# Fused attention and slot network on one core: the first attention's loop runs over pairs of sequences, and the next input is transposed one group earlier

## The reference, cut to what matters

```python
x = x + _L0_attn_a_ref(_layernorm(x, axis=-1), wq, wk, wv, wo)   # x: (16, 256, 128)
...
q = jnp.einsum('bsd,hed->bhse', x, wq)      # the same for k and v
scores = jnp.einsum('bhse,bhte->bhst', q, k) / scale
scores = jnp.where(causal_mask, NEG, scores)
weights = jax.nn.softmax(scores, axis=-1)
heads = jnp.einsum('bhst,bhte->bhse', weights, v)
return concat @ wo.T
```

## Time and profile before

| | |
|---|---|
| median of 3 runs | 973.76 us (971.58 to 976.4) |
| profiled execution | 972.47 us, span 970.7 us |
| PE busy | 799.1 us (82% of the span) |
| DVE, ACT, POOL busy | 682.4, 472.6, 408.9 us |

### The profile page before, as it was taken

One profiled execution on the slowest core, in us unless ns is written; L12 is line 12 of the kernel. 1 busy time (PEld: TensorE's weight loads), 2 busy tenths in 40 slices (PEclk: granted clock), 3 DMA queues, 4 the chain that ended last, 5 costly groups with the idle time before them and its releaser, 6 DMA issues.

```text
span 970.7 us, 25469 instructions
## 1 busy us (share of the span) xinstructions
PE 799.1 (82%) x10228; PEld 614.3 (63%) x10228; DVE 682.4 (70%) x1560; ACT 472.6 (49%) x801; POOL 408.9 (42%) x302
## 2 busy tenths in 40 slices
PE   2899999999999999999995876668888888839655
PEld 1687777877788777877774453534555555525434
DVE  4677666676666766676664776548999999967763
ACT  1667666676666766776661423023333433315220
POOL 1445444444455444454442100018877778851000
PEclk9999999999999999999997977679999999957786
DMA  6000000000000000000000000000111111120002
GB/s 264 2 3 1 0 0 0 0 0 0 0 0 0 0 0 0 0 0 0 1 2 2 1 0 1 1 1 11 17 18 20 22 22 18 20 27 1 1 1 87
DMA packets 71586, 13.17 MB, mean 14 GB/s; under 512 B 66432, under 2 KB 70528, under 8 KB 70912
## 3 DMA queue, kind: packets, MB, share of 16 engines
q1 hardware_dynamic: 71552, 12.71, 6.0%
HBM read 8.51 MB, written 4.19 MB: 13 GB/s over the span
## 4 chain that ended last, share of the span: by engine, by line
PE 67%; DVE 19%; issue 6%; ACT 5%; POOL 3%; DMA 1%; DVEq 0%; SPq 0%; ACTq 0%; POOLq 0%
PE PS L525 6%; PE PS L482 6%; PE PS L341 6%; PE PS L342 5%; PE PS L343 5%; PE PS L418 4%; DVE b_prod L811 4%; PE PS L704 3%; PE PS L518 3%; PE PS L713 3%; PE PS L504 3%; PE PS L508 2%; PE PS L506 2%; PE PS L695 2%; PE PS L489 2%
## 5 line engine op out<-in xcount | busy, mean ns | idle before, releaser
L626 POOL TENSOR_TENSOR a_pl<-a_p,a_ph 128x1024 f16<-128x1024 f32 (+1 forms) x128 | 210.4, 1644 | 273.5 <-ACT a_ph L551 273.5
L858 POOL TENSOR_TENSOR b_w<-b_v,b_e 128x2048 f32<-128x2048 f32 x32 | 137.7, 4306 | 6.8 <-ACT b_e L773 6.8
L548 ACT ACTIVATE a_p<-PS 128x1024 f32<-128x1024 f32 (+1 forms) x128 | 103.8, 811 | 75.6 <-PE PS L489 75.5
L593 DVE TENSOR_REDUCE a_nm<-PS 128x4 bf16<-128x512 f32 (+1 forms) x128 | 121.3, 947 | 0.0
L541 ACT ACTIVATE a_qk_h<-PS 128x512 f16<-128x512 f32 x128 | 73.3, 604 | 79.5 <-PE PS L343 78.6
L551 ACT ACTIVATE a_ph<-PS 128x1024 f16<-128x1024 f32 (+1 forms) x128 | 103.0, 804 | 0.0
L811 DVE TENSOR_TENSOR b_prod<-PS,b_qt 128x512 f32<-128x512 f32 x128 | 83.0, 678 | 15.8 <-PE PS L697 15.0
L341 PE MATMUL PS<-xh,a_wqk_h 128*128 128x256 f16 x256 | 70.8, 277 | 27.1 <-DVE xl L577 26.9
L582 DVE TENSOR_TENSOR a_qk_l<-PS,a_qk_h 128x512 f16<-128x512 f32 x128 | 87.0, 681 | 2.8 <-ACT a_qk_h L541 2.8
L364 POOL TENSOR_TENSOR veps<-mv,eps 128x2 f32<-128x2 f32 (+2 forms) x40 | 7.9, 198 | 189.4 <-DVE mv L1132 137.1
L695 PE MATMUL PS<-b_kh,w_rolls 128*128 128x256 f16 x256 | 64.7, 281 | 20.6 <-DVE b_prod L811 19.7
(11 more groups left out here) (220 smaller groups left out, 2060.7 us busy)
## 6 DMA issues: line engine op xcount, KB each, us to landing
scratch_dram<-b_o SPq DMA_DIRECT2D x32, 64.0 KB, 3.5
b_y<-scratch_dram SPq DMA_DIRECT2D x16, 128.0 KB, 2.1
out_dram<-X SPq DMA_DIRECT2D x2, 1024.0 KB, 3.9
w_rest<-rest_dram SPq DMA_DIRECT2D x1, 1846.0 KB, 14.6
X<-x_dram SPq DMA_DIRECT2D x1, 1792.0 KB, 10.7
w_first<-first_dram SPq DMA_DIRECT2D x1, 1600.0 KB, 6.6
w_rolls<-rolls_dram SPq DMA_DIRECT2D x1, 512.0 KB, 15.2
X<-x_dram SPq DMA_DIRECT2D x1, 256.0 KB, 3.1
```

What stands on the lines that cost most here:

```text
L548: act.activation((a_p0, a_p1)[j][:, me, :, :, :].rearrange("p a h q -> p a (h q)"), TT[:, :, 0:512 - 256 * j], ACT.Exp, scale=EA ** -0.5)
L593: dve.tensor_reduce(a_nm[:, nx, j, :].rearrange("p (a h) -> p a h", a=2)[:, :, 0:2], MM[:, :, 0:256 * (j + 1)].rearrange("p a (h k) -> p a ...
L626: pool.tensor_tensor(*(n[:, g % 2, :, :, :].rearrange("p a h q -> p (a h q)") for n in (pl, p, ph)), ALU.subtract).then_inc(a_split, 1)
L858: pool.tensor_tensor(b_w8[:, j, :, :, :], rolled_values(par, j, 0, H), rolled_exps(par, j, 0, H), ALU.mult).then_inc(b_weighed, 1)
```

## The change

The loop's body becomes a pair of sequences (`a_steps(0) + a_steps(1)`), run 6 times; sequences 0 and 1 stand written out ahead of it, 14 and 15 behind it. In a step, g now runs from 0 to 7, and its high bit is the parity of the sequence. `xh` and `xl` of the first attention become `a_xhs` and `a_xls` with two slots, the sequence's parity choosing the slot. `norm` moves from group 1 to group 0, `apply` from group 2 to group 1, and `xt` from the end of group 2 to the end of group 1, ahead of `project`.

```diff
-def a_steps(first=False, last=False):
+def a_steps(par, first=False, last=False):
...
-        put(g == 2 and not last, ("apply", 0))
+        put(g == 1 and not last, ("apply", 0))
...
-        put(g == 1 and not last, ("norm", 0))
+        put(g == 0 and not last, ("norm", 0))
...
-        put(g == 2 and not last, ("xt", 0))
+        put(g == 1 and not last, ("xt", 0))
         put(g == 1 and not first, ("project", 0))
...
-A_PLAN = [(A_PROLOGUE, -1, None), (a_steps(first=True), 0, None), (a_steps(), 1, NB - 2),
-          (a_steps(last=True), NB - 1, None), (A_EPILOGUE, NB, None)]
+A_PLAN = [(A_PROLOGUE, -1, None), (a_steps(0, first=True) + a_steps(1), 0, None),
+          (a_steps(0) + a_steps(1), 1, NB // 2 - 2), (a_steps(0) + a_steps(1, last=True), NB // 2 - 1, None),
+          (A_EPILOGUE, NB // 2, None)]
...
+        a_xhs, a_xls = sb("a_xhs", [128, 2, SEQ], F16), sb("a_xls", [128, 2, SEQ], F16)
...
+        def parts(b_par, g):
+
+            slot = 1 - b_par if g == GA - 1 else b_par
+            return a_xhs[:, slot, :], a_xls[:, slot, :]
...
-                    act.activation(xh[:, :], src[:, 0:SEQ], ACT.Copy).then_inc(a_xh, 1)
+                    act.activation(a_xhs[:, 1 - b_par, :], src[:, 0:SEQ], ACT.Copy).then_inc(a_xh, 1)
```

More of the change, by code:

```diff
@@ L75, in put @@
         def put(cond, *new):
-            steps.extend((kind, g, n) for kind, n in new if cond)
+            steps.extend((kind, GA * par + g, n) for kind, n in new if cond)
         put(prepare, ("qk", 0), ("qk", 1))
@@ L134, in b_steps @@
     return steps
-A_PROLOGUE = [("norm", 3, 0), ("apply", 3, 0), ("xt", 3, 0), ("qk", 3, 0), ("qk", 3, 1), ("lo", 3, 0),
-              ("lo", 3, 1), ("masks", 3, 0), ("max", 3, 0), ("v", 3, 0), ("vlo", 3, 0), ("masks", 3, 1), ("max", 3, 1)]
+A_PROLOGUE = [("norm", 7, 0), ("apply", 7, 0), ("xt", 7, 0), ("qk", 7, 0), ("qk", 7, 1), ("lo", 7, 0),
+              ("lo", 7, 1), ("masks", 7, 0), ("max", 7, 0), ("v", 7, 0), ("vlo", 7, 0), ("masks", 7, 1), ("max", 7, 1)]
 A_EPILOGUE = [("normal", 0, 0), ("turn", 0, 0), ("pv", 0, 0), ("pv", 0, 1), ("normal", 1, 0), ("turn", 1, 0),
@@ L404, in a_read @@
             kind, g, j = step
+            b, g = 2 * b + g // GA, g % GA
             u = GA * b + g
@@ L420, in causal, with do @@
                               skip_group_check=True)
+        def parts(b_par, g):
+            slot = 1 - b_par if g == GA - 1 else b_par
+            return a_xhs[:, slot, :], a_xls[:, slot, :]
         def a_tensor(pe):
-            def do(step, b, fill):
+            def do(step, i, fill):
                 kind, g, j = step
+                b_par, b, g = g // GA, 2 * i + g // GA, g % GA
                 u = GA * b + g
@@ L439, in do @@
                         pe.wait_ge(a_xl, b + 2)
+                    xh, xl = parts(b_par, g)
                     for z in range(2):
                         ins = mm3(pe, dst[:, z * SEQ:(z + 1) * SEQ], a_wqk_h[:, pair, z, :], a_wqk_l[:, pair, z, :],
-                                  xh[:, :], xl[:, :], z == 0, z == 1)
+                                  xh, xl, z == 0, z == 1)
                     ins.then_inc(a_filled, 1)
@@ L511, in do @@
                 elif kind == "turn":
-                    if isinstance(b, int) and b == 0 and g == GA - 1:
+                    if isinstance(i, int) and b == 0 and g == GA - 1:
                         pe.wait_ge(w_loaded, 16 * 2)
@@ L568, in do @@
                 elif kind == "norm":
-                    if isinstance(b, int) and b == 0:
+                    if isinstance(i, int) and b == 1:
                         dve.wait_ge(x_late, 16)
@@ L576, in do @@
                     dve.wait_ge(a_xh, b + 2)
-                    dve.tensor_tensor(xl[:, :], R[fill.bank][:, 0:SEQ], xh[:, :], ALU.subtract).then_inc(a_xl, 1)
+                    dve.tensor_tensor(a_xls[:, 1 - b_par, :], R[fill.bank][:, 0:SEQ], a_xhs[:, 1 - b_par, :],
+                                      ALU.subtract).then_inc(a_xl, 1)
                 elif kind == "qk":
@@ L610, in do @@
                                       ALU.add).then_inc(a_added, 1)
-            run_plan(dve, A_PLAN, do, chain, 1 + GA)
+            run_plan(dve, A_PLAN, do, chain, 2 * (1 + GA))
             dve.wait_ge(a_added, NB)
         def a_gpsimd(pool, chain):
-            def do(step, b, fill):
+            def do(step, i, fill):
                 kind, g, j = step
+                b_par, b, g = g // GA, 2 * i + g // GA, g % GA
                 u = GA * b + g
@@ L627, in do @@
                                        ALU.subtract).then_inc(a_split, 1)
-            run_plan(pool, A_PLAN, do, chain, 1)
+            run_plan(pool, A_PLAN, do, chain, 2)
         b_filled = sem("b_filled")
```

## The result

The changed kernel took 977.17 us (median of 20 runs, 973.48 to 1015.27) against 973.62 us before (20 runs): 1.0044 of before, 95% interval 1.0029 to 1.0059. It is slightly slower. One of its runs, the 1015 us one, had a granted clock of 0.803 and is left out of the ratio. The profiled execution took 974.43 us at a mean granted clock of 0.925; the other runs stand at 0.904 to 0.922 and mostly take more.

What follows compares the result with a forecast made beforehand. PE was taken to bound the kernel, setting the pace in the first attention. 972.47 - 25.2 (wait) + 5.0 (statistics) + 17.3 (branches) = 969.6 us, stated as 970, range 952 to 979.

Steps and rivals of the forecast that it cites:

- The wait that goes: PE's wait in `qk` for `xl` in the first attention vanishes in 14 sequences, 1.80 us each: 25.2 us less.
- The statistics without cover: In group 0 nothing hides the norm's statistics, so PE's `maxrow` starts 0.36 us later a sequence: 5.0 us more.
- `apply`, POOL and the transposition cost nothing: The other moved steps of DVE, POOL, ACT and PE fit their new groups in the first attention: no cost.
- The sum without branches: Vanished wait plus uncovered statistics in the first attention: -25.2 + 5.0 = -20.2 us, giving 952.3 us.
- The loop's branch: The doubled PE body of 2,061 instructions is not kept; five branches back stall 3.45 us each: 17.3 us more.
- near 80 packets: Decisive sign on PE's instruction queue: near 80 packets if the body is refetched each trip, some 35 if kept.
- one block fetched by one engine after a request: Price of PE's stall at a branch: packet 1.35 us plus small memory read 2.1 us, one after the other, 3.45 us.
- what would make it wrong: Includes a branch stall well under 2 us or over 5, for instance with the block behind the loop's head missing too.
- The rival of the clock: Each branch stall also lowers PE's clock, 1.7 us more a branch: 25.8 us, time 978.0 us; chance 0.17, costlier branches included.
- Today the branch costs nothing: In the loop before the change, PE's matmuls on both sides of the branch start 0.21 us apart, without a gap.
- A kept body: Rival: PE's doubled loop body is fetched once and kept, so branches stay free: 952.3 us; chance 0.28.
- a wait that only moves: Rival: `qk` 0 of group 2 or some `maxrow` waits as long for ACT or DVE: about 972 us; chance 0.05.

Runs made afterwards that it cites:

- head_moved31: The changed kernel with 31 small idle matmuls on PE ahead of everything, moving the loop's head by 62 places: 982.76 us, 1.0085 of before.
- before_unrolled: The kernel before the change with its fourteen looped sequences written out, nothing else changed: 967.68 us, 0.9946 of before.
- head_moved20: The changed kernel with 20 small idle matmuls on PE ahead of everything, moving the loop's head by 40 places: 988.81 us, 1.0154 of before.

## Why the prediction was wrong, point by point

- **The wait that goes**, 14 x 1.80 = 25.2 us: right. Unrolled and with the statistics covered, a sequence falls from 30.40 to 28.51 us, 1.89 less.
- **The statistics without cover**, 0.36 us a sequence: right, 0.35 us in the timeline, 0.37 by experiment. `apply`, POOL and the transposition cost nothing, as said.
- **The sum without branches** was -20.2 us. Without a loop on either side the change brings 967.68 - 947.5 = 20.2 us.
- **The loop's branch**: right that the body is not kept, and near 80 packets were forecast, 84 came. The failing step is its price, 3.45 us as "one block fetched by one engine after a request". The first stop has that size, 2.69 to 3.24 us, and 2.97 to 3.30 where it stands alone (the size is right; of the two times it was added from, the 2.1 us are those of a transfer of 128 KB, not of a small read). But a branch costs more than one block. The block behind the head's must be fetched too, and PE catches up with it (0.82 to 1.38 us more), or the clock falls in that time, and PE is slow while the block comes. Both were named in the forecast, one as a rival and one as what would make it wrong, and neither was in the sum. The measured mean is 4.44 us. 5 x 4.44 = 22.2 us against 17.3 turns the forecast's -2.9 into +2.0, and +2.0 is what the profiled execution shows (974.43 - 972.47). That agreement is partly luck: two sequences fewer are looped (-0.9 us), and by the last `project` the first attention ends 1.1 us earlier than before, so some 3 us lie in the stages behind it, which were not changed (439.8 against 436.8 us). That lies within the 435.5 to 440.1 us that these stages take in the ten kernels; what moves them is open.
- **The rival of the clock** is part of the truth. It fell behind two of five branches in the profiled run, and against the forecast's argument a full PE ahead of the stop did not protect it. Most other runs of the changed kernel have a lower mean clock than the profiled one and take longer, so the median of +3.5 us over before has probably more such falls; those runs have no trace, so this is argued and not shown.
- "Today the branch costs nothing" was right for the branch and wrong for the loop: 0.45 us a sequence. The forecast's sequence of 30.66 us was also misread; it is 30.85. Two adjacent sequences without a stop took 2 x 29.33 = 58.7 us, against 58.4 forecast.
- A kept body (0.28) and a wait that only moves (0.05) did not come about.

## What to carry to other kernels

Ahead of unrolling a loop body by two, count its instructions on each engine and the blocks of 256 that they touch. Where a body here touched more than seven blocks on PE and was fetched anew, each branch back cost 3.0 to 7.6 us, and the gain of a good reordering was gone. Look at the instruction packets first: a number far above the program's own length says that a loop is refetched, and a wait "issue" at its head says what that costs. Here the same reordering was worth 2.1% with a small loop, and 2.1% again with no loop on either side, where leaving the loop gave 0.5% more; code written out in a straight line streamed in for nothing.

## What the runs showed of the hardware

- A refetched loop head stopped PE for 2.7 to 3.3 us. With 50 instructions of its block left, a second stop of 0.8 to 1.4 us followed at 3 of 5 branches of the changed kernel; with about 11 left, one of 1.6 to 2.2 us at all five; with 130 or more left, none. Where the branch stood 25 and 11 places behind a block's start, the first stop was 3.8 to 4.3 us, and in head_moved31 two blocks were moved before PE went on. In before_unrolled, PE's straight-line code drew one packet of 16 KB for 258 instructions on average. The Trainium skill, "Runtime: NRT & Kernel Launch", section "Instruction fetch mechanics", has blocks of 256 instructions and a stall at a branch that leaves what is held; the packets and the places of the stops here agree. Of its 2,048 instructions, 1,869 over eight blocks were not kept.
- Stops of 2.7 to 4.3 us were followed by PE's lower clock (0.50 in single stretches) for some 3 to 7 us, behind 2 of 5 branches in the changed kernel and behind all 5 in head_moved31 and head_moved20. The waits of 1.64 us in the kernel before never were.
- A loop cost 0.45 us for each 30 us of PE's work even where its code was kept (30.85 against 30.40 us a sequence in the kernel before).
